# Scans: the spread of C one state sooner behind GpSimd's states, and the chain to the next rates two slots ahead in the eighth and tenth turns

## The reference, cut to what matters

```
dA = exp(delta * A);  h = h * dA + (delta * u) * B
y  = sum over n of h[d, n] * C[n]
y  = (y + u * D) * silu(z);  out = y @ out_proj
```

## Time and profile before

| | before |
|---|---|
| median of 3 runs | 3140.39 us |
| the profiled execution's own time | 3135.47 us |
| its span | 3133.7 us |
| first scan to last `s_term` of VectorE | 1587.70 to 2320.06 us |
| mean granted TensorE clock | 0.889 |

### The profile page before, as it was taken

The page is one execution under the profiler, slowest core; times in us unless marked ns, Lnnn a source line. Parts: engine busy times, 40 slices in busy tenths (PEclk is TensorE's granted clock), DMA queues, the critical chain, the costliest instruction groups (busy, mean ns, idle before and its releaser), DMA issues. The chain is left out here.

```text
span 3133.7 us, 59098 instructions
## 1 busy us (share of the span) xinstructions
PE 2880.1 (92%) x22949; PEld 1661.3 (53%) x22949; DVE 2174.8 (69%) x4853; ACT 1630.6 (52%) x3273; POOL 1124.1 (36%) x542
## 2 busy tenths in 40 slices
PE   8888899999899999998978998898899889998998
PEld 3333334444799999743434544554453345574547
DVE  5777645655777777776679888878861559926991
ACT  3555553443333333336366777777753557726761
POOL 1111120000200000000078879887930219923991
PEclk8999999999555555699988999999999999999999
DMA  5434414023000000030442333332302001250224
GB/s 154 99 94 103 107 60 123 23 76 102 3 4 4 4 4 4 3 99 13 136 155 89 85 90 99 85 94 87 98 22 105 1 1 81 95 201 6 89 96 200
DMA packets 113495, 234.36 MB, mean 75 GB/s; under 512 B 13761, under 2 KB 50753, under 8 KB 104769
## 3 DMA queue, kind: packets, MB, share of 16 engines
q1 hardware_dynamic: 113216, 230.59, 23.5%
HBM read 185.71 MB, written 44.83 MB: 74 GB/s over the span
## 5 line engine op out<-in xcount | busy, mean ns | idle before, releaser
L1451 PE MATMUL psum<-h_ring,h_parts 128*128 128x4 f16 x12264 | 478.3, 168 | 0.5 <-DVE h_ring L1594 0.4
L2738 DVE TENSOR_TENSOR_SCAN s_hh<-psum,s_dbu 128x512 f32<-128x512 f32 x384 | 445.4, 1204 | 43.8 <-ACT psum L2349 41.0
L2608 POOL TENSOR_TENSOR s_dbu<-s_du,s_bb 128x1024 f32<-128x1024 f32 x191 | 446.5, 2362 | 39.1 <-DVE s_hh L2738 27.6
L1451 PEld LDWEIGHTS psum<-h_ring,h_parts 128*128 128x128 f16 x12264 | 430.6, 106 | 47.6 <-DVE h_ring L1594 0.8
L1513 ACT ACTIVATE h_now<-psum 128x16 f32<-128x16 f32 x1024 | 189.0, 185 | 324.1 <-PE psum L1451 317.2
L2349 ACT ACTIVATE psum<-s_delta,s_decay 128x512 f32<-128x512 f32 x384 | 255.9, 685 | 94.6 <-DVE s_hh L2738 93.0
L2241 PEld LDWEIGHTS psum<-w_c,s_term 128*128 128x128 f32 x1536 | 198.0, 149 | 131.3 <-issue 113.6
L1002 POOL MEMSET r_weights<- 128x512 f32 x4 | 2.1, 526 | 721.1 <-POOLq L1403 511.3
L1594 DVE TENSOR_SCALAR h_ring<-h_now 128x16 f16<-128x16 f32 x1024 | 178.6, 174 | 118.1 <-ACT h_now L1513 77.3
L2241 PE MATMUL psum<-w_c,s_term 128*128 128x128 f32 x1536 | 231.5, 286 | 5.0 <-ACT s_y L2428 4.7
L1596 DVE SCALAR_TENSOR_TENSOR h_ring<-h_now,h_ring 128x16 f16<-128x16 f32 x1024 | 179.4, 175 | 35.2
(11 more groups left out here) (585 smaller groups left out, 6235.6 us busy)
## 6 DMA issues: line engine op xcount, KB each, us to landing
s_bb<-s_wide SPq DMA_DIRECT2D x192, 256.0 KB, 3.6
x_spill<-x_flip SPq DMA_DIRECT2D x28, 1024.0 KB, 3.8
f_share<-f_wide SPq DMA_DIRECT2D x208, 128.0 KB, 3.2
s_cc<-s_wide SPq DMA_DIRECT2D x60, 256.0 KB, 3.4
a_ks<-a_spread SPq DMA_DIRECT2D x96, 128.0 KB, 3.3
a_qs<-a_spread SPq DMA_DIRECT2D x96, 128.0 KB, 3.9
x_spare<-x_spill SPq DMA_DIRECT2D x4, 2048.0 KB, 11.9
x_raw<-x_spill SPq DMA_DIRECT2D x4, 2048.0 KB, 10.8
```

The source lines that it names most:

```text
L1451: mm = nc.tensor.matmul(here[:, cols], parts[:, part, GROUP * grp + p, :], ring[:, (i - 1) % RING, grp, cut, cols], start=False, stop=True ...
L2608: nc.gpsimd.tensor_tensor(dbu[:, s % D_RING], du[:, t % 2], both(bb[:, s % B_RING, :]), ALU.mult).then_inc(dbu_ready, 1)
L2738: nc.vector.tensor_tensor_scan(hh[:, s % 4, half, :], DECAYS[i % 3], dbu[:, s % D_RING, half, :], 0.0, ALU.mult, ALU.add).then_inc(scan_do ...
```

## The change

`pick_c` moves in TensorE's program. Behind a state of GpSimd's it is issued at the end of the state before (one state sooner), except in a lent state, where it is issued in the middle of its own state, before `add_up`'s first half. Other states keep their place. In turns 7 and 9 the whole chain is two slots (one state) earlier on TensorE, ScalarE and GpSimd, `squash` too (15 to 13), GpSimd takes states 10 and 11 instead of 11 and 12, `inputs` moves from state 13 to 12, and so the lent state is 12.

```diff
     def late(t):
-        return 3 if t == FIRST else 0
+        return {FIRST: 3, 7: -2, 9: -2}.get(t, 0)
     def pool_states(t):
         if t == FIRST:
             return (0, 3, 6, 13, 14)
+        if t in (7, 9):
+            return (0, 3, 6, 10, 11)
         return (0, 3, 6, 11, 12) if prepares(t) else (0, 4, 5, 9, 12)
+    def lent(s):
+        return s // N + 1 < TURNS and s % N == rate_slot(s // N) // 2 + 2
+    def ahead(s):
+        return s > 0 and not by_vector(s - 1) and not lent(s)
     def squash_slot(t):
         if prepares(t):
-            return SLOTS * t + (14 + late(t) if late(t) else 15)
+            return SLOTS * t + (17 if t == FIRST else 15 + late(t))
@@ TensorE's loop
                         beside(2 * s)
+                    if s < STEPS and lent(s):
+                        pick_c(s)
                     if s >= 3 and s != STEPS:
                         add_up(s - 3, 0)
...
-                    if s < STEPS and by_vector(s):
-                        pick_c(s)
+                    if s < STEPS and by_vector(s) and not ahead(s):
+                        if not lent(s):
+                            pick_c(s)
+                    elif s + 1 < STEPS and by_vector(s + 1) and ahead(s + 1):
+                        pick_c(s + 1)
@@ GpSimd's loop
-                    if t + 1 < TURNS and n == (13 if prepares(t) else 7):
+                    if t + 1 < TURNS and n == (12 if t in (7, 9) else 13 if prepares(t) else 7):
                         inputs(t + 1)
```

## The result

| | before | after |
|---|---|---|
| median (runs), us | 3137.10 (7) | 3148.93 (7) |
| lowest to highest | 3133.85 to 3140.45 | 3143.17 to 3154.77 |
| ratio | | 1.0034, 95% interval 1.0022 to 1.0047 |
| the same kernels in a later set | 3138.60 (35) | 3145.27 (12), 1.0021 (1.0006 to 1.0035) |

The predicted time was 3137.5 us, in a range from 3125 to 3145; 3148.93 us is outside it, on the side to which 0.13 was given. The medians stand 11.8 us apart in the first set and 6.7 us in the second; the ratios make it some 10.7 and 6.6 us. Three executions in all, 3844.92 and 6582.14 us of the kernel e9 and 3375.04 us of the kernel before, lay far above the rest and enter no ratio.

The account below looks back on a forecast made before the run. TensorE and VectorE hand the stage to and fro, neither full, with TensorE's work setting its full stretches. Gains 2.9, waits 0.5 and chain loss 0.4 us made 2.8 us less than the profiled 3135.47; against the median 3137.5 us, range 3125 to 3145.

Parts of the forecast that it names:

- What bounds the stage: Whole stage: neither TensorE nor VectorE is full; in TensorE's full stretches its sum of work sets the time.
- Spreads where TensorE is full: (8, 1) and seven like waits: the next ordinary spread does not move, so 0 gained; upper end 14.5 us for the seven.
- (0, 1): Turn 0, state 1: spread ahead of `mid`, next scan limited by its decay; gain 0.75 us, from 0 to 1.55.
- (4, 6): Turn 4's lent state: spread moves ahead of half an `add_up`; TensorE's pause before (4, 7) comes back, gain 0.49 us.
- (11, 1): Turn 11, state 1: a wait of 1.12 us goes, the next spread limits the gain to 0.57 us.
- (9, 12): Turn 9's lent state, formerly 13: a wait of 0.85 us goes, the next term can come 0.57 us sooner.
- (7, 12): Turn 7's lent state, formerly 13: a TensorE pause of 0.49 us comes back, gain 0.49 us.
- The new waits: Moved `pick_c` waits for VectorE's term at 12 places, 7.8 us together; charged 0.5 us, between 0 and 1.3.
- (5, 1): Turn 5, state 1: longest new wait, 2.7 us, taken up by TensorE's pause of 2.38 us behind it.
- The moved chain: Turns 7 and 9, two slots ahead: -0.4 us (loss) for turn 7, gain 1.0 less 0.6; 0 for turn 9.
- The clock: Slow spells in TensorE's full stretches: 0, with 1.7 us either way for each of two spells near the moved rates.
- Rival B: Early `pick_c` blocks TensorE, dense matmuls reach ScalarE late and decays queue: slower by 8.2 us, 3148.6 us, chance 0.12.

Follow-up runs that it names:

- e9: Kernel before with only the spreads behind GpSimd's states one state sooner, lent spreads and both chains as before: ratio 1.0012 to before.
- e15: Kernel before with lent spreads moved and turn 7's chain two slots sooner, convolution behind the gate's matmul, ScalarE's gate before `keep_conv`: ratio 0.9994 to before.
- e7: Kernel before with only the lent states' spreads moved to mid-state, both chains as before: ratio 0.9985 to before, 0.9994 in a second set.
- e13: Kernel before, unchanged, run again as if changed: ratio 0.9999 to before, stage 2.5 us longer.
- e8: Changed kernel, but turn 7 has gate's matmul before convolution and ScalarE's gate before `keep_conv`, turn 9 product's matmul before `mean`: ratio 1.0006 to before.
- e4: Changed kernel, but in turn 7 ScalarE does the gate's activation ahead of `keep_conv`, TensorE's order as changed: ratio 1.0027 to before.

## Why the prediction was wrong, step by step

- **What bounds the stage** (neither engine full, TensorE's full stretches set the sum): right. Turn 4 kept TensorE's 60.3 us, and of the 11.6 us fewer waits before terms most stood before scans instead.
- **Spreads where TensorE is full, 0**: right in kind. (8, 1) to (8, 2) went as written (a wait of 2.29 us, not 2.81, but the term at the same time), and the waits grew at the next ordinary spread or before scans.
- **(0, 1), gain 0.75**: counted from (0, 1), (0, 3) came 0.78 us sooner, but at (0, 15) 0.72 us were given back. "VectorE is what runs on from there, so it stays" failed, and turn 1 started 0.13 us later, not 0.7 us sooner.
- **(4, 6) and (11, 1), 0.49 and 0.57**: turn 4 is 0.46 shorter, which is luck in part: the lent spread alone brings 0.62 to 0.84, and the spreads behind GpSimd's states take 0.45 of it. Turn 11 wins 0.77. **(9, 12), 0.57, and (7, 12), 0.49**: right in kind and a little low, 0.71 (e15) and 0.88 (e7 against e13), with the chain in its old place.
- **The new waits**: their sum (7.8 us, 8.0 found in e9) was right, and their price was not. I charged 0.5 because most are under 0.45 us; where TensorE is full, even 0.48 us at (5, 4) comes back whole, and 1.36 at (9, 4) cost 1.03 (in e9). I had asked only whether a wait is long, not whether a pause stands behind it. Where I did ask, at (5, 1), the answer was right. Spreads ahead alone are +2.8 to +4.5 us in the stage where 0.5 less 1.3 was forecast, though the unchanged kernel itself moves by 2.5.
- **The moved chain, the step that failed most**: -0.4 for turn 7 and 0 for turn 9. The places were named (`keep_conv` ahead of the gate, `mean` ahead of the product) but priced as work that moves, 0.6 us for an instruction's length and "up to 0.8". What moved was a wait: 3.16 us on ScalarE, 2.59 to 2.98 us on TensorE. Measured at a full clock: +3.84 at (7, 6) and +1.42 at (9, 2); net, turn 7 is 2.2 us longer than the unchanged kernel's at the same clock and turn 9 2.36. The order of two pairs of matmuls makes 2.1 and 1.4 us of that (after against e8). For turn 7 I named ScalarE's order; e4 and e8 show that it was TensorE's, where the convolution waits for GpSimd.
- **The clock, 0 with 1.7 us for each of two spells**: too narrow. The unchanged kernel moves by 3.07 us in one turn. The profile that I forecast from held a low stretch in turn 7 that costs 1.68 us and is not in its repeat.
- **Rival B** put the loss into evictions behind an early `pick_c`; half of it, the queue behind a waiting matmul, is what happened, but mostly by the chain.

What can be given to the change, at like clocks, is: turn 4 -0.46, turn 5 +0.5, turn 6 some +0.5, turn 7 +2.2, turn 9 +2.36, turn 11 -0.77, together +4.3 us. It is a sum of readings from single profiles, and those of turns 5 and 6 are taken from e9, whose low stretches lie about as before's do. Turn 10's 3.03, turn 3's 1.05 and the other 1.6 of turn 5 go with where the clock was low. The rest of the loss of some 7 to 11 us lies outside the stage or in where the low stretches fall, and is not settled: outside it the profiled executions differ from 2396.5 to 2407.0 us though all kernels are alike there.

## What to carry to other kernels

When a dependent matmul is issued earlier in an in-order engine's program, price the wait of its input at the new place, not its own length, and then ask who waits for the matmuls behind it. A wait in front of a stretch without pauses came back here, short as it was, and one in front of a pause was free (0.48 us cost, 2.6 us did not). Before reading 3 us out of two profiles, profile the unchanged kernel twice, and look whether the granted clock was low in the same places: half of the largest single effect in these runs, 2.87 us, was a matmul pair at 1.2 GHz.

## What the hardware showed that I had not expected

- The clock can fall to 1.2 GHz amid full work. In before it was low from 2066.42 to 2069.83 us, while TensorE was busy 28.80 of 28.80 us from 2047.8 to 2076.6; in e13 it was low for 6.8 us in turn 10 (6.80 busy of 6.80 at 0.50). The places change from one execution of the same program to the next: e13 has no low stretch in the full part of turn 7, and before none over the rates of turn 10. What one costs hangs on the place: 3.07 us over the rates of turn 10, 1.68 in turn 7, 1.43 in turn 8.
- Where the low stretches fall alike, the executions repeat to 0.04 us per turn of 60 us (turns 0, 1, 2, 4, 5 and 9 of e13 against before), so an edit of 0.5 us can be read turn by turn where 12 timed runs can't resolve it.
